# A GNN layer and a sliced-attention layer on one core: rows of x in triples, and whole MLP layers placed in the edge stage by a table of batches

## The reference

```python
aggr = segment_sum(edge_attr, dst, 6250)
h = relu(concat([layernorm(x), aggr]) @ W1 + b1)
h = relu(h @ W2 + b2)
x = x + h @ W3 + b3
n = layernorm(x)
fx, xm = n @ W_fx + b_fx, n @ W_x + b_x              # 8 heads of 64
w = softmax((xm @ W_slice + b_slice) / clip(temperature), axis=-1)
token = (fx^T w) / (sum_n w + 1e-5)                   # per head, 64 slices
out_slice = softmax(q k^T / 8) v                      # of the tokens
x = x + (out_slice spread back by w) @ W_out + b_out
```

## Time and profile before

| what | us |
| --- | --- |
| median of three runs | 666.78 |
| lowest and highest | 665.12, 671.9 |
| the profiled execution | 664.12 |
| its span in the profile | 662.3 |

### The profile page before, as it was taken

How to read it: one execution, slowest core, us unless ns; L and a number is a source line. 1 busy time by engine, 2 the same in 40 slices (tenths; PEclk the granted TensorE clock), 3 DMA queues, 4 the chain that set the end, 5 groups by cost and what they waited for, 6 DMA issues and landing times.

```text
span 662.3 us, 11868 instructions
## 1 busy us (share of the span) xinstructions
PE 603.9 (91%) x3481; PEld 363.9 (55%) x3481; DVE 398.1 (60%) x1104; ACT 284.9 (43%) x422; POOL 243.8 (37%) x330
## 2 busy tenths in 40 slices
PE   5787777899999899999998899999999998899997
PEld 2455555566644344443897544444444443688886
DVE  6744444455455555443588888888888888422221
ACT  5234444455422223232200245455455455677773
POOL 3235344434200000000123466666666666234441
PEclk9789999999999999999999999999999999999999
DMA  8999999999999999991100053343333344021121
GB/s 305 364 403 403 388 398 403 397 386 386 348 379 382 387 384 387 386 322 38 41 7 0 32 78 66 65 78 63 69 74 63 68 75 79 17 79 70 73 79 70
DMA packets 107142, 133.97 MB, mean 202 GB/s; under 512 B 57595, under 2 KB 59601, under 8 KB 107109
## 3 DMA queue, kind: packets, MB, share of 16 engines
q1 hardware_dynamic: 106293, 133.29, 59.6%
q10 hardware_dynamic: 816, 0.26, 0.2%
HBM read 114.29 MB, written 6.40 MB: 182 GB/s over the span
## 4 chain that ended last, share of the span: by engine, by line
PE 68%; DMA 20%; DVE 5%; issue 4%; SPq 2%; POOL 1%; DVEq 0%; ACT 0%; POOLq 0%
DMA ring_mem<-edge_attr_in 20%; PE ps L1529 13%; PE ps L1442 13%; PE ps L1459 12%; PE ps L1214 10%; PE ps L1251 6%; PE ps L1257 5%; PE ps L1373 2%; PE ps L1317 2%; PE ps L1435 2%; PE ps L1245 1%; DVE x_sb L1010 1%; DVE bn L1014 1%; SPq L390 1%; SPq L396 0%
## 5 line engine op out<-in xcount | busy, mean ns | idle before, releaser
L1214 PE MATMUL ps<-ring_mem,side 128*32 128x256 f32 (+1 forms) x1596 | 105.2, 398 | 35.5 <-DMA ring_mem<-edge_attr_in 35.4
L934 DVE TENSOR_TENSOR big<-big,ps 128x64 f32 x319 | 70.8, 222 | 89.6 <-PE ps L1245 40.6
L1442 PE MATMUL ps<-ring_mem,xn 128*128 128x512 f32 x196 | 93.3, 599 | 1.0 <-DVE ring_mem L1095 0.7
L1459 PE MATMUL ps<-side,ring_mem 128*128 128x512 f32 x196 | 92.3, 593 | 1.9 <-ACT ring_mem L742 1.9
L1214 PEld LDWEIGHTS ps<-ring_mem,side 128*32 128x32 f32 (+1 forms) x1596 | 51.0, 113 | 74.0 <-issue 44.2
L631 POOL TENSOR_TENSOR ring_mem<-ring_mem 128x512 f32<-128x512 f32 x49 | 67.2, 1372 | 30.7 <-DVE ring_mem L1095 30.1
L1529 PE MATMUL ps<-side,ring_mem 128*128 128x256 f32 x360 | 77.9, 379 | 0.0
L699 ACT ACTIVATE side<-ps 128x512 f32<-128x512 f32 (+1 forms) x50 | 25.5, 510 | 119.8 <-PE ps L1214 119.5
L1529 PEld LDWEIGHTS ps<-side,ring_mem 128*128 128x128 f32 x360 | 68.4, 190 | 9.3
L757 ACT ACTIVATE ring_mem<-ring_mem 128x512 f32<-128x512 f32 x49 | 30.9, 630 | 91.3 <-POOL ring_mem L624 91.3
L802 ACT ACTIVATE ring_mem<-big 128x1024 uint16 (+1 forms) x45 | 60.7, 1358 | 15.6 <-PE ps L1529 15.6
(11 more groups left out here) (136 smaller groups left out, 814.5 us busy)
## 6 DMA issues: line engine op xcount, KB each, us to landing
ring_mem<-edge_attr_in SPq DMA_DIRECT2D x84, 1024.0 KB, 8.6
ring_mem<-edge_attr_in SPq DMA_DIRECT2D x62, 256.0 KB, 5.5
x_sb<-x_in SPq DMA_DIRECT2D x24, 256.0 KB, 5.7
result<-ring_mem SPq DMA_DIRECT2D x24, 256.0 KB, 2.0
big<-side SPq DMA_TRANSPOSE x49, 3.0
side<-L_gnn_W_in SPq DMA_DIRECT2D x2, 256.0 KB, 6.2
ring_mem<-L_ffn_W_x_in SPq DMA_DIRECT2D x2, 256.0 KB, 3.7
ring_mem<-L_ffn_W_out_in SPq DMA_DIRECT2D x1, 512.0 KB, 3.8
```

What stands on the lines that cost most here:

```text
L934: dve.tensor_tensor(win, win, found[:, :, q * WINDOW:(q + 1) * WINDOW], ALU.add).then_inc(groups_added, 1)
L1214: return mm(ps[q * WINDOW:(q + 1) * WINDOW, SUM_BANKS[h], col:col + F], lhsT=hot[0:parts, h * 2 + j, t, :], rhs=ring8[0:parts, h * 2 + j, ...
L1442: last = mm(ps[:, 4 + k, :], lhsT=xn[:, r, k * P:(k + 1) * P], rhs=soft[:, r, :], start=isinstance(t, int) and t == 3, stop=isinstance(t, ...
L1459: last = mm(ps[:, s % 2, :], lhsT=xn_t[:, s % 2, k, :], rhs=wc[:, k, :], start=(k == 0), stop=(k == KF - 1))
```

## The change

Rows of x are loaded, normalised and run through the first layer in triples of tiles: `TRIPLES` is 16, and one tile is left. So the x work needs batches 0 to 19 instead of 0 to 27. It uses banks 4 to 7.

From batch 20 on a table of batches says which single item of the MLP a batch does: a whole tile of layer 1 (11 of them, `L1_AT`), of layer 2 (10, `L2_AT`), or a triple of tiles of layer 3 (9, `L3_AT`). Banks are 4 and 5 in even batches, 6 and 7 in odd ones. For a third-layer batch VectorE does the residual add before its window adds, and the statistics after them. `w3_sb` takes the place of `w1a_sb` and is loaded in batch 21. The tail has the other 22 tiles of layer 3, in seven triples and one tile.

The statistics of all tiles go to `mv2`; GpSimd makes the pow of the first 30 tiles in one step. `base_i`, `mx`, `sm`, `rc` and `rstd2` get other memory. The far path, taken only where edges lie outside their window, is made to fit.

At the end GpSimd adds b_out into `x_sb` itself, in triples, all 17 steps in a row, and VectorE adds the projection into `x_sb`, from which triples are stored; its first output add waits for all 17 steps.

```diff
-X_TRIPS = 13
-
-H1E_AT = {10: 0, 11: 1, 13: 2, 15: 3, 16: 4, 18: 5, 19: 6, 20: 7, 22: 8, 23: 9, 24: 10}
-H2_AT = {12: 0, 14: 1, 15: 2, 17: 3, 18: 4, 20: 5, 21: 6, 22: 7, 23: 8, 24: 9}
+X_TILES = 3
+X_TRIPS = 10
...
+L1_AT = {20: 0, 21: 1, 25: 2, 29: 3, 32: 4, 35: 5, 38: 6, 40: 7, 43: 8, 45: 9, 48: 10}
+L2_AT = {22: 0, 23: 1, 27: 2, 31: 3, 34: 4, 37: 5, 41: 6, 42: 7, 46: 8, 47: 9}
+L3_AT = {24: 0, 26: 1, 28: 2, 30: 3, 33: 4, 36: 5, 39: 6, 44: 7, 49: 8}
...
+def bank_of(b):
+
+    return 4 + 2 * (b % 2)
```

```diff
-                if what == "x" and before(b, X_PAIRS):
+                if what == "x" and before(b, TRIPLES):
                     if past(b, 1):
                         sp.wait_ge(x_in, b * 16)
-                    sp.dma_start(tiles_of(b * 2, 2).rearrange("p t f -> p (t f)"),
-                                 x[bass.ds(b * (2 * P), 2 * P), :].rearrange("(p t) f -> p (t f)", p=P)
+                    sp.dma_start(tiles_of(b * X_TILES, X_TILES).rearrange("p t f -> p (t f)"), rows_of(x, b, X_TILES)
                                  ).then_inc(x_in, 16)
...
+            with sp.Fori(0, TRIPLES) as i:
+                sp.wait_ge(y_ready, i * X_TILES + X_TILES)
+                sp.dma_start(rows_of(out, i, X_TILES), tiles_of(i * X_TILES, X_TILES).rearrange("p t f -> p (t f)")
+                             ).then_inc(y_out, 16)
```

```diff
+            FIRST = X_TILES * (L3_TRIPLES + 1)
+            rstd(0, 0, FIRST, FIRST)
             pool.wait_ge(fold_t, 1)
...
             pool.wait_ge(late_in, 16 * 10)
-            pool.wait_ge(att_t, 11)
-
-            def residual(t, s, i):
-                if past(t, UNROLL):
-                    pool.wait_ge(y_ready, t - UNROLL + 1)
-                pool.tensor_tensor(xo[:, s, :], x_sb[:, bass.ds(t, 1), :].rearrange("p a f -> p (a f)"),
-                                   bout_bc, ALU.add).then_inc(xo_ready, 1)
-
-            run_steps(pool, residual, TILES, 1, MLP_CHUNKS - 1)
+
+            def add_b_out(i, n):
+                pool.tensor_tensor(tiles_of(i * X_TILES, n), tiles_of(i * X_TILES, n),
+                                   bout_bc.unsqueeze(1).broadcast_to([P, n, F]), ALU.add).then_inc(xo_ready, 1)
+
+            with pool.Fori(0, TRIPLES) as i:
+                add_b_out(i, X_TILES)
+            add_b_out(TRIPLES, 1)
```

```diff
-                if isinstance(i, int) and i in H1E_AT:
-                    dve.wait_ge(h1x_ready, 4 * (H1E_AT[i] + 1))
-                    add_h1e(H1E_AT[i], h)
+                if isinstance(b, int) and b in L1_AT:
+                    dve.wait_ge(h1x_ready, 2 * (TRIPLES + 1))
+                    add_h1e(L1_AT[b], bank_of(b))
+                if isinstance(b, int) and b in L3_AT:
+                    dve.wait_ge(xb3_ready, TRIPLES + 1)
+                    residual(L3_AT[b], L3_AT[b], X_TILES, bank_of(b))
                 if h == 0:
...
+                if isinstance(b, int) and b in L3_AT:
+                    residual_stats(L3_AT[b], L3_AT[b], X_TILES, X_TILES * (L3_AT[b] + 1))
...
                 dve.wait_ge(y_psum, t + 1)
-                dve.wait_ge(xo_ready, t + 1)
-                if past(t, UNROLL):
-                    dve.wait_ge(y_out[s // 2], i * 16)
-                dve.tensor_tensor(o_sb[:, s, :], ps[:, s, 0:F], xo[:, s, :], ALU.add).then_inc(y_ready, 1)
+                if isinstance(t, int) and t == 0:
+                    dve.wait_ge(xo_ready, TRIPLES + 1)
+                dve.tensor_tensor(of_tile(t), ps[:, s, 0:F], of_tile(t), ALU.add).then_inc(y_ready, 1)
```

```diff
+                if isinstance(b, int) and b in L1_AT:
+
+                    pe.wait_ge(w1b_in, 16)
+                    pe.wait_ge(groups_added, sums_ahead(b * 2, groups) + CREDIT)
+                    banks_free(b)
+                    for m in range(KF):
+                        first_layer_edges(L1_AT[b], m, bank_of(b)).then_inc(h1e_psum, 1)
+                if isinstance(b, int) and b in L2_AT:
                     pe.wait_ge(w2_in, 16)
...
+                    pe.wait_ge(h1_ready, L2_AT[b] + 1)
+                    banks_free(b)
+                    for m in range(KF):
+                        last = second_layer(L2_AT[b], m, ps[:, bank_of(b) + m, :], 4 * P)
+                    last.then_inc(l2_psum, 1)
+                if isinstance(b, int) and b in L3_AT:
+                    pe.wait_ge(w3_in, 16)
+                    hidden_ready(L3_AT[b])
+                    banks_free(b)
+                    third_layer(L3_AT[b], X_TILES, bank_of(b)).then_inc(l3_psum, 1)
                 turn(b, h, groups)
```

`banks_free(b)` waits for the reader of the banks of batch b - 2, `hidden_ready(i)` for the second layers that triple i needs. The tail, from the last turn on:

```diff
+            i = L3_TRIPLES
+            pe.wait_ge(h1e_added, 2 * L1_TILES + 1)
+            full_layer3(i, 4)
             layer2(MLP_CHUNKS - 2, 4 * P, [ps[:, m, :] for m in range(KF)])
             pe.wait_ge(groups_added, CREDIT + ALL_SUMS)
...
+            pe.wait_ge(x2_ready, i + 1)
+            full_layer3(i + 1, 4)
+            fold_transposes()
             pe.wait_ge(h1e_added, 2 * MLP_CHUNKS + 1)
...
+            full_layer3(i + 2, 6)
...
+            full_layer3(i + 3, 4)
             fold_weights()
...
+            pe.wait_ge(x2_ready, i + 3)
+            full_layer3(i + 4, 6)
             fold_biases()
...
+            third_layer(TRIPLES, 1, 3).then_inc(l3_psum, 1)
+            pe.wait_ge(x2_ready, i + 4)
+            full_layer3(TRIPLES - 2, 4)
```

More of the change, by code:

```diff
@@ L81, in run_batches @@
     trip(1, 2, P, "x")
-    with eng.Fori(2, TWOS // UNROLL) as i:
+    with eng.Fori(2, X_TRIPS - 2) as i:
         trip(i, 2, P, "x")
-    for i in range(TWOS // UNROLL, TRIPS):
-        trip(i, 4, P if i < FOURS // UNROLL else LAST_P, "x" if i <= X_TRIPS else "")
+    for i in range(X_TRIPS - 2, TRIPS):
+        trip(i, 2 if i < TWOS // UNROLL else 4, P if i < FOURS // UNROLL else LAST_P, "x" if i < X_TRIPS else "")
 def run_steps(eng, step, total, peel_front, loop_trips):
@@ L491, in _ @@
             with sp.If(far > 0):
+                sp.wait_ge(mv2_ready, X_TILES * L3_TRIPLES)
+                for i in range(L3_TRIPLES):
+                    sp.dma_start(tiles_of(i * X_TILES, X_TILES).rearrange("p t f -> p (t f)"), rows_of(x, i, X_TILES)
+                                 ).then_inc(gen_x_in, 16)
                 with sp.Fori(0, TWOS) as c:
@@ L555, in _ @@
             for a, first in enumerate((TWOS, FOURS)):
-                for tile, at, n in H1E_RUNS:
-                    pool.iota(steps_of[:, a, tile:tile + n], [[UNROLL, n]], base=UNROLL * at - first, channel_multiplier=-1,
+                for tile, at, step, n in L1_RUNS:
+                    pool.iota(steps_of[:, a, tile:tile + n], [[2 * step, n]], base=2 * at - first, channel_multiplier=-1,
                               allow_small_or_imprecise_dtypes=True).then_inc(lowest_ready, 1)
@@ L561, in _, with ln_triple @@
             pool.wait_ge(consts, 6)
[L563 to L572 removed]
+            def ln_triple(i, n):
+                pool.wait_ge(mv1_ready, i * X_TILES + n)
                 if past(i, 1):
[L574 removed]
+                    pool.wait_ge(xn1_ready, i * X_TILES)
                 pool.tensor_tensor(var_e[:, 0:n], mv1[:, 0:n, 1], eps[:, 0:n], ALU.add)
@@ L606, in _, with rstd @@
-            for i in range(3):
-                rstd_chunk(i, i, 4, i * 4 + 4)
+            def rstd(step, t, n, seen):
+                to = rstd2[:, bass.ds(t, n)]
+                pool.wait_ge(mv2_ready, seen)
+                pool.tensor_tensor(to, mv2[:, bass.ds(t, n), 1], eps[:, 0:1].broadcast_to([P, n]), ALU.add
+                                   ).then_inc(var2_ready, 1)
+                pool.wait_ge(var2_ready, step + 1)
+                pool.tensor_tensor(to, to, half[:, 0:1].broadcast_to([P, n]), ALU.pow).then_inc(rstd2_ready, 1)
@@ L1045, in _ @@
             inv_all = inv_temp.unsqueeze(2).broadcast_to([P, H, G])
-            dve.wait_ge(xb3_ready, X_PAIRS + 1)
-            for i in range(4):
-                full_residual(i, i % 2)
+            full_residual(L3_TRIPLES + 2, 6)
+            full_residual(L3_TRIPLES + 3, 4)
             dve.wait_ge(fold_t, 2)
@@ L1057, in _ @@
             fold_step(dve.tensor_tensor(heads(c_bc), heads(c_bc), inv_all, ALU.mult))
-            with dve.Fori(3, MLP_CHUNKS // 2 - 1) as j:
-                for a in range(2):
-                    full_residual(j * 2 + a, a)
             def normalise(t, s):
@@ L1356, in _ @@
                     last.then_inc(gen_l2, 1)
-                pe.wait_ge(gen_h2, H2_TILES + 1)
+                pe.wait_ge(gen_h2, L2_TILES + 1)
+                for i in range(L3_TRIPLES):
+                    if i > 0:
+                        pe.wait_ge(gen_x2, i)
+                    third_layer(i, X_TILES, 2).then_inc(gen_l3, 1)
+                pe.wait_ge(gen_x2, L3_TRIPLES)
             def layer2(i, cols, halves):
@@ L1364, in layer2, with full_layer3 @@
                 last.then_inc(l2_psum, 1)
-            def layer3(step, i, n, bank):
-                if past(step, 2):
-                    pe.wait_ge(x2_ready, step - 1)
-                for a in range(n):
-                    for k in range(KF):
```

(10 more changed lines are left out.)

404 lines of the change are left out of this document (193 added, 211 removed).

## The result

| | before | changed |
| --- | --- | --- |
| median of four runs each, us | 666.22 | 675.2 |
| lowest and highest | 665.12, 671.9 | 671.88, 676.07 |
| the profiled execution | 664.12 | 676.07 |
| its span in the profile | 662.3 | 674.3 |

The changed kernel takes 1.0148 times as long (95% interval 1.0114 to 1.0182), that is 1.5% more. 675 with a range of 662 to 685 was predicted. The two profiled executions lie 12.0 us apart, the medians 9.0; the sum of the prediction was made against the profiled one and gave +9.4. So I go through the stages there; against the profiled executions the forecast is 2.6 us short, and the close agreement of 675 with 675.2 rests in part on this, that the profiled execution of before lies 2.1 us under its median and that of after 0.9 over.

What follows compares the result with a forecast made beforehand. Edge loads set the pace up to batch 19, TensorE mostly after. Edge stage +21.3, tail -26.8 and -0.4, output +13.3 and +2 give +9.4 on 664.1, so 673.5; stated 675 us, range 662 to 685.

Steps and rivals of the forecast that it cites:

- Batches: Edge stage from batch 20: a batch with a first- or second-layer tile takes 5.94 us, with a third-layer triple 5.1.
- slower than 0.22 us each: Sign against the forecast: third-layer matmuls, with their stride of three, take longer than 0.22 us each.
- Stage 1: Edge stage up to batch 20: loads still hide the wider x work, but 1.3 MB more is loaded, +3.3 us.
- The waits before the first layers: Edge stage: first layers stand behind VectorE's window adds of the batch before, 1.13 to 2.75 us each, 20.1 in all.
- T: The end of the previous turn, from which the forecast counts the start of first layers and window adds.
- if third layer, second layer, first layer follow each other: Edge stage: the triple's statistics and two one-hots push the window adds to T + 3.5; first layer waits 1.8 us.
- Rival A: Edge stage: VectorE keeps ahead, so first-layer waits are 10 us instead of 20; 665 us in all, chance 0.17.
- Rival C: Clock drops after four edge-stage waits of 2.5 us and over, +8, and output restarts slower; 685 us, chance 0.12.
- The tail: Last turn to first logits: 27 third-layer tiles fewer and VectorE's bound gone, 36.9 us instead of 63.7, -26.8.
- The output stage: Fifth projected tile waits until all 17 b_out adds are done, +13.3 us; slower clock on restart, +2.
- B: Output stage: GpSimd's wide b_out adds finish before TensorE's fourth projected tile and hide; 661 us, chance 0.12.
- D: Edge and output stages: neither wait appears, the tail's gain stands against the added work alone; 650 us, chance 0.04.

Runs made afterwards that it cites:

- run 1: Changed kernel, but GpSimd adds b_out tile by tile and each VectorE output add waits only for its own tile: 663.07 us, ratio 0.9966 to the kernel before.
- run 3: Changed kernel, but edge-stage first layers read settled x tiles, not window sums, so skip that wait (different output): 654.64 us, ratio 0.9838 to the kernel before.
- run 5: Changed kernel with both b_out added tile by tile and window adds ahead of the item's result: 655.44 us, ratio 0.9871 to the kernel before.
- run 6: Changed kernel, but the nine third-layer triples and residuals of the edge stage go back to the tail: 681.08 us, ratio 1.0257 to the kernel before.
- run 2: As run 1, but GpSimd starts its b_out adds only when attention is nearly over: 662.51 us, ratio 0.9961 to the kernel before.
- run 4: Changed kernel, but VectorE adds windows before the MLP item's result, and ScalarE's first ReLU comes a batch later: 668.39 us, ratio 1.004 to the kernel before.
- run 7: As run 5, but without third layers and residuals in the skipped far block: 656.6 us, ratio 0.9872 to the kernel before.
- run 8: As run 5, but in the 11 first-layer batches TensorE turns the sums before the layer: 651.5 us, ratio 0.9801 to the kernel before.

## Why the prediction was right

The forecast, slower by the two new waits less the gain of the tail, holds, and runs 1, 3 and 5 show it by taking the waits away: 12.1 us for one, 20.6 for the other with its clock. By the prediction's own steps:

- **Batches.** 5.94 and 5.1 us were forecast, 5.93 and 5.16 measured. A triple took 166.07 - 163.31 = 2.76 us, 0.23 a matmul instruction, so the sign "slower than 0.22 us each" did come, at a price of 9 x 0.06 = 0.5 us. The stride of three lengthens the weight loads (mean 254 ns in L1356, against 202 with the stride of two in the kernel before), but with the same loads a triple in the tail took 2.59 to 2.66, so that they are the cause is not shown.
- **Stage 1** was put at +3.3 and came to +1.8. "Some 38" tiles was too few for the kernel before: by 132.5 us it had issued 21 of its pairs. The DMA engines moved 50.7 MB up to batch 20 before and 51.5 in the changed kernel (24 us at 326 and 108.5 at 395 GB/s; 24 at 324 and 110.3 at 396). The 0.8 MB between them, instead of 1.3, are 2.0 us at 401 GB/s.
- **The waits before the first layers** were mis-sized. By kind: 2.40, 2.52 and 2.38 for 2.75; 1.65 for 1.65; 1.07 and 1.06 for 1.13; 1.71 for 2.5 in batch 21, whose layer started 4.25 us after T for the 4.37 worked out, but whose own sums waited for a load and ended later. The step most off is the 1.8, "if third layer, second layer, first layer follow each other": it measured 1.12, 1.39 and 1.12. VectorE's backlog was mostly worked off by then: in batch 31 the adds began 0.27 us after the turn (214.45 against 214.18), where T + 3.5 means 0.8. The 1.39 has another reason: ahead of the adds of batch 34, an even one, VectorE idles 0.76 us, about what the register load takes elsewhere (0.84). Sum 16.4 for 20.1. Rival A, 10 us, is out.
- **Rival C came true in part.** Three idles of 2.4 to 2.5 us in or right behind the edge stage were followed by a stretch at the lower clock, of 1.7 us each; a fourth, 2.38 at 299.05, was not. So its sum of +8 was too high and my zero too low. Against it I had argued from idles of 1.6 us and less, which said nothing on 2.4.
- **The tail** gave 3.1 less than forecast. The step that failed is "with the order followed step by step the first logits come 36.9 us after the stage": it leaves out the idle of 2.42 us, at which the trace shows a load of instructions (below), and the clock behind it, 1.7 us. Without these 4.1 it would have been 35.9.
- **The output stage** came to +15.0 for +15.3. The adds were 29.2 for 29.9, and the fifth tile came 31.2 us after the start of the memsets for 593.0 - 560.4 = 32.6. The +2 for the restart measured 3.1.
- **Rivals B and D** needed the b_out adds to hide. As the change has them they don't; added by tile they do (run 1), but that is another kernel. D's 650 does not follow from the sum: 675 less 20.1 and 15.3 is 640.
- **The signs.** Three of those named for "right" did not come as stated: the waits make 16.4 us and not 18 to 22, the gap in the projection is 7.9 and not 12 to 14, and the first logits come at 368.3 and not near 364. The reasons are those above.
- Two errors of size nearly cancel: 3.7 too many for the waits, and the clock's 3.4 not counted. Such cancelling is luck, and so is a part of the agreement with 675.2, as said above; the range of 669 to 681 for the forecast's own case is what the steps really bore.

That third layers in the edge stage are hidden I had not priced by itself. Run 6 shows that 24.8 us of matmuls moved there bring 5.9 to 7.2 us. It fits that the loads bound this stage almost as closely as TensorE (172.75 of 175 us busy and a DMA share of 0.98 in run 3).

**What stays open.** The idle of 2.4 us between the last turn and the first triple of the tail is in the changed kernel and in runs 1 to 5, 7 and 8, whatever the waits, the b_out order or the length of the far block; in run 6, whose last batch carries no third layer, it is missing (turn at 313.64, third layer at 314.17). The waits name no releaser, but the DMA queues of the changed kernel show something there. The row is for 328.2 to 328.4 us, the last turn ending at 328.35 (queue and kind: packets, MB, share of the time of the 16 DMA engines):

```profile
q8 instruction: 1, 0.02, 30.2%
```

One load of instructions (16 KB) starts at the turn's end; from 310 to 328.25 there is none, and one at 308.8 us came while TensorE worked on. All eight kernels with the idle have such a load within 0.1 us of that point (in run 7 at 321.17, the turn ending at 321.20). Run 6 has none from 309 to 316 us. So I now take the idle for TensorE's wait for its instructions behind the branch over the far block. The queue does not say whose instructions it loads, and no run moves this load alone, so the cause is argued, not shown. It would also fit run 7: a shorter block changes nothing as long as the code behind it is not loaded yet. With the clock behind it the idle is worth up to 4 us.

## What to carry to other kernels

When a change moves work to an earlier stage, ask which wait now has nothing in front of it: the first layers' waits were in the kernel before too, and half layers ran in their place. Where one instruction waits for another engine, put what is ready ahead of it, on both sides of the wait: the adds ahead of the residual, the turn ahead of the layer and b_out tile by tile turned a change that costs 1.5% into one that saves 2%. And where each step of one engine needs only its own step of another, a wait for the last of 17 holds it for the whole block: here 12 us, though GpSimd needs 29 us for all tiles and the projection more than 80.
